# Tile 0's lists move into the step loop, the second batch's lists ahead of it, and an output tile goes behind the sum

## The chip, the cores and the metric

The kernel runs on one core of a Trainium2 chip. The metric is the device time in microseconds of one execution. Before the change it is 549.84 us, the median of 3 runs (545.92, 549.84, 549.85). The execution that was profiled took 548.86 us, of which 547.1 us lie between the first and the last instruction.

## The reference

One layer of a graph transformer over 4096 nodes of 256 features. The mask is sparse (adjacency plus the diagonal) and its density falls with the node number, so tile 0 (nodes 0 to 127) has by far the most neighbours.

```python
mask = adj.astype(float32) + eye(n)
q = (h @ Wq.T + bq).reshape(n, 8, 32)      # k and v the same way
scores = einsum('nhd,mhd->hnm', q, k) / sqrt(32)
scores = where(mask == 0, -1e9, scores)
ctx = einsum('hnm,mhd->nhd', softmax(scores), v).reshape(n, 256)
h1 = layer_norm(h + ctx @ Wo.T + bo)
ff = relu(h1 @ W1.T + b1) @ W2.T + b2      # 256 -> 1024 -> 256
h2 = layer_norm(h1 + ff)
```

## The kernel before, in words

**Stages.** The kernel first projects keys and values of all 4096 nodes on TensorE, 16 pairs of tiles (`project_kv`), and stores them to a table in HBM through the POOL and ACT queues. Queries are projected pair by pair (`project_q`) and stored to 16 small tables by the SP queue. Meanwhile VectorE looks for the neighbours in the adjacency rows (`find_dve` for most tiles, `find0_dve` for tile 0). A neighbour list is a few slots for each unit, a range of columns; neighbours beyond the slots spill to rows of other partitions.

**Batches and steps.** Every batch but tile 0's is one step of the loop over `STEPS`: 19 steps, the first four with one tile each, then pairs of tiles in steps 4 to 15, then three single tiles in 16 to 18. b0 and b1 are the first two batches. Tile 0 (`TILE0`, 14 units) is not a step: its pieces are spread over later steps (gathers from step 6, scores in steps 8 to 14, softmax in step `SOFTMAX0` = 15, weights in `WEIGHTS0` = 16, its sum in `SUM0` = 17).

**Lists.** Before a batch can gather, a chain over three engines makes its spill lists: `spill_dve`, then `starts_pe` (one small matmul), `distance_act`, `rt_dve`, `lists_pe` (one matmul for each unit), `cols_dve`, which gives the row numbers in `col_of`; only then can the POOL queue issue `gather_edges` and `gather_queries` (indirect DMAs). In the loop, step i makes the lists of step i+1. Before the change b1's lists are made in step 0, and tile 0's lists are made whole between the projections and step 0.

**A step.** VectorE multiplies gathered queries and keys (`edge_scores_dve`, L636 to L643), then the own scores; TensorE spreads the edge scores to their rows (`ell_pe`, L850); VectorE masks and takes the maximum, ScalarE the exponential, TensorE sends tops and sums back (`tr_pe`, L858), VectorE weights the values (`edge_weight_dve`, L741), TensorE sums them (`sum_pe`, L876 and L879), ScalarE moves the context out (`ctx_act`, L989). VectorE also finds the neighbours of step i+2.

**Dense work.** From step 4 on (`FIRST_JOB`) the layers behind the attention run in the gaps of the steps, one job of four tiles for two steps. The even step (place 0) has the attention output `post_pe_attn` (L1101), the odd step (place 1) the relu halves `post_pe_ff` (L1121) and two of the four output tiles `post_pe_out` (L1134); the other two come in the even step that follows. `dense(gap)` is what a gap holds; `outs_own` says which output tiles the odd step holds and where. `post_act_x` (L1145) adds a bias to the residual of the next job and stands behind `ctx_act` in the odd step; `post_pe_attn` waits for it.

Each engine runs its own instruction list in program order; semaphores tie them together. So a wait holds up all that stands behind it on that engine.

Of the kernel before, what the change touches and what calls it, by code (L numbers as in the profile page):

```python
# [5 lines left out]
ALU = mybir.AluOpType  # L6
# [7 lines left out]
P = 128  # L14
# [72 lines left out]
def batches():  # L87
# [12 lines left out]
    for p, q in enumerate(other[:1] + [q for q in out if q.first] + other[1:]):  # L100
# [18 lines left out]
SUM0 = NB - 2  # L119

# [25 lines left out]
def build(nc, xT, adj, wqkvT, bq, bk, bqkv, woT, w1T, w2T, cols, g2, be2, out):  # L146
    with ExitStack() as ctx:
# [193 lines left out]

        psum0 = sem("psum0")
# [42 lines left out]
        def job(g, first_tile, at, bank, signals):  # L385
# [33 lines left out]
         s_gprobs, s_gpt_ps, s_gpt, s_gpv, s_grl, s_gctx, s_gctxT_ps, s_gctxT) = [sem(n) for n in (  # L419
            "s_gkt s_gmask s_gdiag s_gqt_ps s_gqt s_gscores s_gmax s_gnm "  # L420
            "s_gprobs s_gpt_ps s_gpt s_gpv s_grl s_gctx s_gctxT_ps s_gctxT").split()]
# [165 lines left out]
        def starts0_dve(dve):  # L587

            q = TILE0
            dve.wait_ge(starts_ps, q.p + 1)  # L590
            nc.vector.scalar_tensor_tensor(units(mids, q), ps[:, SMALL, 0:q.U], -2.0, units(spill, q), ALU.mult, ALU.add
                                           ).then_inc(starts_ready, 1)

        def rt_dve(dve, q):
            dve.wait_ge(distance, 2 * q.p + 1)
# [5 lines left out]
        def cols_dve(dve, q):  # L601

            got = lists_out(q)
            dve.wait_ge(lists_ps, q.p + 1)
            base = (q.tiles[0] // 2) * 2 * P
            if q.first:
                nc.vector.tensor_scalar(row_of[q.par][:, 0:q.U], got[:, :, q.k + 1], -1.0 - base, 0.0, ALU.add, ALU.max)
                nc.vector.tensor_copy(row0, got[:, :, q.k + 1])
            else:

                nc.vector.tensor_scalar(row_at[q.par][:, 0:q.U], got[:, :, q.k + 1], -0.5 - base, None, ALU.add)
            nc.vector.tensor_tensor(hot(q), slot_minus_edge[:, 0:q.k].unsqueeze(1).to_broadcast([P, q.U, q.k]),
                                    got[:, :, q.k:q.k + 1].to_broadcast([P, q.U, q.k]), ALU.is_equal).then_inc(hot_ready, 1)
            dve.wait_ge(hot_ready, 2 * q.p + 1)
            wait(dve, cols_ready, q.p)
            pick = picked[:, 0:q.U * q.k].rearrange("p (u k) -> p u k", k=q.k)
            nc.vector.tensor_tensor(pick, hot(q), got[:, :, 0:q.k], ALU.mult).then_inc(hot_ready, 1)
            dve.wait_ge(hot_ready, 2 * q.p + 2)
# [3 lines left out]
        def onehot0_dve(dve):  # L622

            q = TILE0
            dve.wait_ge(cols_ready, q.p + 1)
# [199 lines left out]
        def starts_pe(pe, q):  # L825
            pe.wait_ge(spill_ready, q.p + 1)
            wait(pe, starts_ready, q.p)
            wait(pe, distance, 2 * q.p)
            if q.b == 1 and not q.first:
                pe.wait_ge(cols_ready, TILE0.p + 1)  # L830
            nc.tensor.matmul(ps[:, SMALL, 0:q.U], minus_before[:], units(spill, q), start=True, stop=True).then_inc(starts_ps, 1)

        def lists_pe(pe, q):
            pe.wait_ge(rt_ready, q.p + 1)
            pe.wait_ge(distance, 2 * q.p + 2)
            wait(pe, cols_ready, q.p)
# [47 lines left out]
        def queries0_pe(pe, i):  # L884
# [3 lines left out]
            pe.wait_ge(rt_ready, q.p + 1)  # L888
# [38 lines left out]
        def distance_act(act, q):  # L927

            if not q.first:
# [107 lines left out]
        def gather_edges(pool, q, us=None):  # L1037
            pool.wait_ge(cols_ready, q.p + 1)
            kv_ready(pool)
            if q.first:  # L1040
                queries_ready(pool, q)
# [374 lines left out]
        def outs_own(place, gap):  # L1416
            return {(1, 3): (0, 1)}.get((place, gap), ())
# [646 lines left out]
```

## Time and profile before

| What | Value |
|---|---|
| Median of 3 runs | 549.84 us |
| Profiled execution, span | 548.86 us, 547.1 us |
| TensorE matmuls busy | 475.1 us (87%) |
| VectorE busy | 388.5 us (71%) |
| GpSimd busy | 269.2 us (49%) |
| ScalarE busy | 215.6 us (39%) |
| Mean granted TensorE clock | 0.935 |

Busy time is what an engine spent in its instructions; the granted clock is given as a share of the full 2.4 GHz, so 0.5 is 1.2 GHz. In a timeline a row is a start, a duration, engine, line, operation, shape and count; brackets give the idle time of the engine just before, and what ended it. TensorE is busy nearly always between 158 us and 426 us, and less so between 69 us and 158 us, which holds the end of the projections and steps 0 to 3.

### The profile page before, as it was taken

Reading aid. Unit: us, or ns where it says so; the run is one execution under the profiler, and the core shown is the slowest. Engines: PE = TensorE matmul, PEld = TensorE weight load, DVE = VectorE, ACT = ScalarE, POOL = GpSimd, SP = SyncE. Lnnn points to the kernel's source line nnn. Section 1 sums busy time; section 2 is a strip of 40 time slices with the busy share of each in tenths; the row PEclk is TensorE's granted clock in tenths of the full one; section 3 lists DMA queues with packets and bytes.
Section 4 is the critical chain, followed back from the end, with each engine's and each line's share of the span. In section 5 each row is a group of like instructions: output and inputs, shape, how many; then the busy total and the mean of one; then the engine's idle time right before and its main releaser. Section 6 shows DMA issues by size and latency. Waiting matters only on the chain.

```text
span 547.1 us, 7365 instructions
## 1 busy us (share of the span) xinstructions
PE 475.1 (87%) x2274; PEld 373.5 (68%) x2274; DVE 388.5 (71%) x1067; ACT 215.6 (39%) x533; POOL 269.2 (49%) x374
## 2 busy tenths in 40 slices
PE   5999959588266989999999999999999499989893
PEld 4888858476255478668758857957856487668682
DVE  0258837479968687889989989998978779653103
ACT  1234243324223533633562463362463434422530
POOL 7544342435414526677656667645546264600502
PEclk9999978989557998999999999999999789999997
DMA  7999748969997979999998998994856323310101
GB/s 179 295 269 324 214 162 192 192 197 237 211 285 135 250 133 192 226 163 241 177 222 196 133 228 170 193 222 111 189 142 118 91 88 112 92 40 1 40 0 42
DMA packets 42571, 91.66 MB, mean 168 GB/s; under 512 B 4888, under 2 KB 20632, under 8 KB 42400
## 3 DMA queue, kind: packets, MB, share of 16 engines
q0 software_dynamic: 16512, 55.60, 52.9%
q1 hardware_dynamic: 24224, 33.69, 17.7%
q10 hardware_dynamic: 1792, 1.85, 1.0%
q8 instruction: 20, 0.33, 0.2%
q14 instruction: 23, 0.19, 0.1%
HBM read 123.09 MB, written 16.80 MB: 256 GB/s over the span
## 4 chain that ended last, share of the span: by engine, by line
PE 56%; DVE 15%; issue 9%; DMA 8%; POOL 5%; ACT 5%; SPq 1%; POOLq 0%; ACTq 0%; DVEq 0%
PE ps L1121 16%; PE ps L1134 14%; DMA xT_all<-in_xT 6%; PE ps L1101 6%; PE ps L1796 5%; PE ps L1089 2%; DVE slots L732 2%; PE ps L876 2%; DVE adj_bytes L531 2%; PE ps L1812 2%; PE ps L850 2%; DVE adj_bytes L535 2%; PE ps L879 1%; DMA work<-q_table,row_of 1%; POOL slots L1044 1%
## 5 line engine op out<-in xcount | busy, mean ns | idle before, releaser
L1134 PE MATMUL ps<-w,xT_all 128*128 128x256 f32 x512 | 118.8, 385 | 4.3 <-ACT xT_all L1171 2.6
L1121 PE MATMUL ps<-xT_all,w 128*128 128x512 f32 (+1 forms) x288 | 117.9, 554 | 2.6 <-ACT xT_all L1171 1.4
L1134 PEld LDWEIGHTS ps<-w,xT_all 128*128 128x128 f32 x512 | 96.0, 192 | 18.0 <-ACT xT_all L1171 3.8
L1044 POOL DMA_INDIRECT slots<-kv_table,col_of x54 | 52.7, 977 | 91.0 <-DVE col_of L620 75.0
L1121 PEld LDWEIGHTS ps<-xT_all,w 128*128 128x128 f32 x288 | 52.3, 192 | 47.2 <-issue 40.1
L1034 POOL DMA_INDIRECT slots<-kv_table,found x48 | 50.6, 1055 | 44.0 <-PE ps L879 21.0
L1171 ACT ACTIVATE xT_all<-ps,col_table 128x512 f32<-128x512 f32 (+1 forms) x72 | 45.8, 641 | 59.2 <-PE ps L1121 58.3
L1796 PE MATMUL ps<-early,xT_all 128*128 128x256 f32 x256 | 59.4, 393 | 6.9 <-DMA early<-in_wqkvT 6.3
L1796 PEld LDWEIGHTS ps<-early,xT_all 128*128 128x128 f32 x256 | 49.7, 197 | 14.8 <-DMA xT_all<-in_xT 4.7
L531 DVE MAX8 adj_bytes<-adj_bytes 128x8 f32<-128x1024 f32 (+5 forms) x40 | 38.2, 974 | 16.1 <-DMA adj_bytes<-in_adj 16.1
L1052 POOL DMA_INDIRECT work<-q_table,row_of x40 | 42.3, 1058 | 13.8 <-issue 13.8
L1191 DVE BATCH_NORM_STATS2 stats<-ps 128x6 f32<-128x256 f32 x62 | 22.2, 419 | 29.8 <-PE ps L1089 29.8
L1101 PE MATMUL ps<-wo,xT_all 128*128 128x256 f32 x128 | 39.6, 438 | 4.1 <-issue 4.1
L989 ACT ACTIVATE xT_all<-ps,col_table 128x256 f32<-128x256 f32 (+1 forms) x38 | 14.4, 431 | 70.1 <-PE ps L879 70.0
L535 DVE FIND_INDEX8 adj_bytes<-adj_bytes 128x8 uint32<-128x1024 f32 (+5 forms) x40 | 39.0, 981 | 0.0
L1230 POOL TENSOR_TENSOR rstd<-mv,eps_col 128x4 f32<-128x4 f32 (+1 forms) x17 | 5.8, 342 | 67.2 <-DVE mv L1197 66.8
L1812 PE MATMUL ps<-early,xT_all 128*128 128x256 f32 x128 | 37.7, 421 | 1.1 <-ACT slots L1647 1.1
L876 PE MATMUL ps<-work,slots 128*128 128x128 f32 x160 | 29.0, 293 | 10.3 <-DVE slots L741 8.5
L1557 POOL TENSOR_TENSOR slots<-slots,early 128x512 f32<-128x512 f32 x16 | 20.2, 1263 | 30.7 <-ACT slots L1647 30.7
L876 PEld LDWEIGHTS ps<-work,slots 128*128 128x128 f32 x160 | 24.6, 205 | 12.0 <-DVE slots L741 9.9
L1647 ACT COPY slots<-ps 128x1024 f32<-128x1024 f32 x16 | 16.2, 1012 | 41.6 <-PE ps L1796 41.6
L1101 PEld LDWEIGHTS ps<-wo,xT_all 128*128 128x128 f32 x128 | 25.6, 222 | 7.2 <-issue 4.6
(178 smaller groups left out, 854.9 us busy)
## 6 DMA issues: line engine op xcount, KB each, us to landing
adj_bytes<-in_adj POOLq DMA_DIRECT2D x31, 512.0 KB
kv_table<-slots POOLq DMA_DIRECT2D x7, 1024.0 KB, 12.8
xT_all<-in_xT SPq DMA_DIRECT2D x13, 512.0 KB, 31.5
slots<-kv_table SPq DMA_DIRECT2D x12, 512.0 KB
out_dram<-early SPq DMA_DIRECT2D x7, 512.0 KB
q_own<-q_table SPq DMA_DIRECT2D x12, 256.0 KB
slots<-in_adj SPq DMA_DIRECT2D x1, 2048.0 KB, 24.8
q_table<-slots SPq DMA_DIRECT2D x8, 256.0 KB, 6.6
```

What stands on the lines that cost most here:

```text
L531: nc.vector.max(top_words[:, u, :], words[:, lo:hi]).then_inc(hunt, 1)
L535: last = nc.vector.max_index(word_at[:, u, :], top_words[:, u, :], words[:, lo:hi])
L876: nc.tensor.matmul(to, edge_slots(q)[:, c, feats], onehot[q.par][:, c, :], start=(u == 0), stop=False)
L1034: nc.gpsimd.indirect_dma_start(to, None, kv_dram, bass.IndirectOffsetOnAxis(ap=idx, axis=0)).then_inc(got_aligned[q.par], 16)
L1044: nc.gpsimd.indirect_dma_start(edge_slots(q)[:, u, :], None, kv_dram, bass.IndirectOffsetOnAxis(ap=col_of[q.par][:, u:u + 1], axis=0)).the ...
L1052: nc.gpsimd.indirect_dma_start(q_edge[q.par][:, u, :], None, q_dram[q.no // 2], bass.IndirectOffsetOnAxis(ap=row_of[q.par][:, u:u + 1], ax ...
L1101: nc.tensor.matmul(to, q["ctxT"][:, k, j * P:(j + 1) * P], wo[:, k, :], start=(k == 0), stop=False)
L1121: last = nc.tensor.matmul(ps[:, q["bank"] + f % 2, 0:q["g"] * P], w1[:, k, f * P:(f + 1) * P], q["h1T"][:, k, :], start=(k == 0), stop=(k ...
L1134: nc.tensor.matmul(to, q["ffT"][:, f, j * P:(j + 1) * P], w2[:, f, :], start=(f == 0), stop=False)
L1171: nc.scalar.activation(q["ffT"][:, f, :], ps[:, q["bank"] + f % 2, 0:q["g"] * P], ACT.Relu, bias=bias_1[:, f:f + 1]).then_inc(q["ff"], 1)
L1796: last = nc.tensor.matmul(ps[:, kv_bank(i, part), j * D:(j + 1) * D], xT_all[:, c, k, r * P:(r + 1) * P], wqkv[:, k, (1 + part) * D:(2 + p ...
L1812: nc.tensor.matmul(to, xT_all[:, c, k, r * P:(r + 1) * P], wqkv[:, k, 0:D], start=(k == 0), stop=False)
```

## The change

Five things are changed. (1) b1's lists are made during the projections, so that the gathers of b0 and b1 are issued one after the other. (2) Tile 0's lists are made in steps 3 (`LISTS0`) to 5 with a semaphore of their own, `lists0`, and in another PSUM bank; VectorE's search of tile 0 stays where it was. (3) `project_q(0)` goes behind the last `project_kv`, and one adjacency load goes from step 0 to the projections. (4) In odd steps the second of two output tiles goes behind `sum_pe`. (5) Tile 0's softmax goes ahead of the search in step 15, its `tr0_pe` to the end of step 15, half of its weighting and both halves of its sum to step 17.

```diff
-    for p, q in enumerate(other[:1] + [q for q in out if q.first] + other[1:]):
+    for p, q in enumerate(other[:2] + [q for q in out if q.first] + other[2:]):
+LISTS0 = 3
         def outs_own(place, gap):
-            return {(1, 3): (0, 1)}.get((place, gap), ())
+            return {(1, 3): (0,), (1, 4): (1,)}.get((place, gap), ())
@@ sync @@
             load_own(sp, STEPS[0])
-            sp.wait_ge(got_edges[STEPS[0].par], 2 * STEPS[0].U * 16)
-            store_q(1)
             load_own(sp, STEPS[1])
-            for i in range(2, Q_BEFORE):
+            for i in range(1, Q_BEFORE):
                 store_q(i)
@@ gpsimd @@
-                if c == 4:
-                    load_adj(pool, c)
+                if c in (4, 6):
+                    load_adj(pool, STEPS[4].h + c // 6)
             gather_aligned(pool, STEPS[0])
+            gather_edges(pool, STEPS[1])
+            gather_queries(pool, STEPS[1])
+            gather_aligned(pool, STEPS[1])
...
-                if i == 0:
-                    load_adj(pool, STEPS[4].h + 1)
@@ scalar @@
-                if i == 13:
-                    take_q(0)
-            distance_act(act, TILE0)
+                if i == 12:
+                    distance_act(act, b1_)
+                    mask_act(act, b1_)
             store_kv(PAIRS - 2)
             store_kv(PAIRS - 1)
+            take_q(0)
+            rows_act(act, b1_)
+            onehot_act(act, b1_)
...
+                if i == SOFTMAX0:
+                    probs0_act(act)
                 edge_exp_act(act, q)
...
                 ctx_act(act, q)
-                if i == SOFTMAX0:
-                    probs0_act(act)
...
+                if i == LISTS0:
+                    distance0_act(act)
@@ tensor @@
-                if i == 13:
-                    project_q(0)
+                if i == 11:
+                    starts_pe(pe, b1_)
                 if i == 14:
-                    starts_pe(pe, TILE0)
-            for i in range(1, Q_LISTS):
-                project_q(i)
-            lists_pe(pe, TILE0)
-            project_q(Q_LISTS)
-            starts_pe(pe, b1_)
-            for i in range(Q_LISTS + 1, Q_BEFORE):
+                    lists_pe(pe, b1_)
+            for i in range(Q_BEFORE):
                 project_q(i)
...
+                if i == LISTS0:
+                    starts0_pe(pe)
...
                 starts_pe(pe, STEPS[i + 2])
+                if i == LISTS0 + 1:
+                    lists0_pe(pe)
+                if i == SOFTMAX0:
+                    tr0_pe(pe)
...
-                if i == SUM0:
-                    sum0_pe(pe, 0)
...
+                tr_pe(pe, q)
                 if i == SUM0:
-                    sum0_pe(pe, 1)
-                if i == WEIGHTS0:
-                    tr0_pe(pe)
-                tr_pe(pe, q)
+                    for k in range(KC):
+                        sum0_pe(pe, k)
@@ vector @@
+                if i == 3:
+                    find_dve(dve, b1_, 0)
+                    columns_dve(dve, b1_)
+                    spill_dve(dve, b1_)
...
+                if i == 12:
+                    rt_dve(dve, b1_)
                 if i == 13:
                     listed0_dve(dve)
                     spill_dve(dve, TILE0)
-            find_dve(dve, b1_, 0)
-            starts0_dve(dve)
-            columns_dve(dve, b1_)
-            spill_dve(dve, b1_)
+            cols_dve(dve, b1_)
             find_dve(dve, STEPS[2], 0)
-            rt_dve(dve, TILE0)
-            cols_dve(dve, TILE0)
-            onehot0_dve(dve)
...
+                if i == LISTS0:
+                    starts0_dve(dve)
                 norm_probs_dve(dve, q)
+                if i == WEIGHTS0 + 1:
+                    weight0_dve(dve, 1)
+                if i == SOFTMAX0:
+                    own0_dve(dve)
+                    below0_dve(dve)
...
+                if i == SOFTMAX0:
+                    norm0_dve(dve)
                 edge_below_dve(dve, q)
                 own_sum_dve(dve, q)
                 edge_weight_dve(dve, q)
-                if i == SOFTMAX0:
-                    own0_dve(dve)
-                    below0_dve(dve)
+                if i == LISTS0 + 1:
+                    rt0_dve(dve)
+                if i == LISTS0 + 2:
+                    cols0_dve(dve)
                 if i == WEIGHTS0:
                     weight0_dve(dve, 0)
-                    weight0_dve(dve, 1)
...
-                if i == SOFTMAX0:
-                    norm0_dve(dve)
```

The POOL queue behind the last key and value store, before the change. `col_of` rows are edge gathers, `row_of` query gathers, `found` rows the gathers of a tile's own first slots.

```order
L1044 DMA slots<-kv_table,col_of 128x512 x2
L1052 DMA work<-q_table,row_of 128x256 x2
L1034 DMA slots<-kv_table,found 128x512 x4
L1070 DMA adj_bytes<-in_adj 128x4096
L1044 DMA slots<-kv_table,col_of 128x512 x2
L1052 DMA work<-q_table,row_of 128x256 x2
L1070 DMA adj_bytes<-in_adj 128x4096
```

The same place of the POOL queue after the change.

```order
L1093 DMA slots<-kv_table,col_of 128x512 x2
L1101 DMA work<-q_table,row_of 128x256 x2
L1081 DMA slots<-kv_table,found 128x512 x2
L1093 DMA slots<-kv_table,col_of 128x512 x2
L1101 DMA work<-q_table,row_of 128x256 x2
L1081 DMA slots<-kv_table,found 128x512 x2
L1119 DMA adj_bytes<-in_adj 128x4096
```

b1's edge and query gathers now stand directly behind b0's, and only one adjacency load is left among them.

VectorE in step 15, from the reciprocal of the step's own softmax on, before the change. `scores` rows of 1800 elements are tile 0's.

```order
L698 TENSOR_TENSOR own_p<-scores,top_rec 128x2x8x2
L531 MAX adj_bytes<-adj_bytes 128x8 x3
L535 MAX_INDEX adj_bytes<-adj_bytes 128x8 x3
L710 TENSOR_TENSOR p_edge<-s_edge,ps 128x16
L719 TENSOR_TENSOR slots<-slots,own_p 128x4x256
L732 TENSOR_TENSOR slots<-slots 128x2x256
L738 SCALAR_TENSOR_TENSOR p_edge<-p_edge,ps 128x16
L741 TENSOR_TENSOR slots<-slots,p_edge 128x2x256
L778 TENSOR_TENSOR slots<-slots,q_own 128x256
L780 TENSOR_REDUCE scores<-slots 128x8
L787 TENSOR_REDUCE top_rec<-scores 128x8
L789 TENSOR_TENSOR scores<-scores,top_rec 128x1800
```

The same place after the change.

```order
L746 TENSOR_TENSOR own_p<-scores,top_rec 128x2x8x2
L826 TENSOR_TENSOR slots<-slots,q_own 128x256
L828 TENSOR_REDUCE scores<-slots 128x8
L835 TENSOR_REDUCE top_rec<-scores 128x8
L837 TENSOR_TENSOR scores<-scores,top_rec 128x1800
L533 MAX adj_bytes<-adj_bytes 128x8 x3
L537 MAX_INDEX adj_bytes<-adj_bytes 128x8 x3
L843 TENSOR_REDUCE total_p<-scores 128x8
L845 RECIPROCAL top_rec<-total_p 128x8
L847 TENSOR_TENSOR scores<-scores,top_rec 128x8
L758 TENSOR_TENSOR p_edge<-s_edge,ps 128x16
L767 TENSOR_TENSOR slots<-slots,own_p 128x4x256
```

Tile 0's softmax now stands ahead of the step's own weighting of values (L741 before; L789 now, three rows behind this excerpt), for which `sum_pe` waits.

## Rows read from the trace of the kernel before

**Rows 1.** The page: busy time of TensorE, and the chain that ended last.

```profile
PE 475.1 (87%) x2274; PEld 373.5 (68%) x2274; DVE 388.5 (71%) x1067; ACT 215.6 (39%) x533; POOL 269.2 (49%) x374
PE 56%; DVE 15%; issue 9%; DMA 8%; POOL 5%; ACT 5%; SPq 1%; POOLq 0%; ACTq 0%; DVEq 0%
```

**Rows 2.** Busy by stretch: engines, TensorE clock, DMA share, GB/s.

```profile
124.00:158.00 34.00, 17.17 (x90) 14.65 (x89) 29.89 (x83) 12.45 (x41) 15.49 (x17) 0.70 1.02 248
...
250.00:295.00 45.00, 43.39 (x216) 32.96 (x216) 41.49 (x97) 20.52 (x52) 30.69 (x32) 1.00 0.95 199
...
426.00:458.00 32.00, 24.33 (x135) 21.53 (x134) 25.97 (x61) 12.03 (x30) 12.81 (x14) 0.84 0.31 91
```

**Rows 3.** VectorE's timeline: end of tile 0's lists, steps 0 to 4.

```profile
84.22 2.83 DVE L627 TENSOR_SCALAR work<-row_mid,adj_bytes 128x128 f32<-128x128 f32 x14
86.97 0.68 DVE L636 TENSOR_TENSOR work<-work,slots 128x512 f32<-128x512 f32 x1
...
101.08 0.23 DVE L580 SCALAR_TENSOR_TENSOR idx_all<-found,row_ids 128x16 f32<-128x16 uint32 x1
107.04 0.69 DVE L636 TENSOR_TENSOR work<-work,slots 128x512 f32<-128x512 f32 x1 [5.73 <-DMA work<-q_table,row_of]
...
123.07 0.69 DVE L636 TENSOR_TENSOR work<-work,slots 128x512 f32<-128x512 f32 x1 [0.58 <-DMA work<-q_table,row_of]
...
156.84 0.69 DVE L636 TENSOR_TENSOR work<-work,slots 128x512 f32<-128x512 f32 x1 [2.55 <-DMA work<-q_table,row_of]
```

**Rows 4.** POOL's timeline: first and last gathers of b0, b1 and step 2.

```profile
76.08 1.10 POOL L1044 DMA_INDIRECT slots<-kv_table,col_of  x1 [5.14 <-DMA kv_table<-slots]
...
95.49 0.99 POOL L1044 DMA_INDIRECT slots<-kv_table,col_of  x1 [8.91 <-DVE col_of L620]
...
99.43 1.42 POOL L1052 DMA_INDIRECT work<-q_table,row_of  x1 [0.30 <-issue]
...
119.26 1.05 POOL L1052 DMA_INDIRECT work<-q_table,row_of  x1 [0.30 <-issue]
```

**Rows 5.** TensorE's timeline: tile 0's 28 list matmuls, and 28 of its sum.

```profile
76.60 6.16 PE L838 MATMUL ps<-first_idx,work 128*128 128x18 f32 x28 [4.53 <-DVE work L598]
...
467.72 3.37 PE L920 MATMUL ps<-work,slots 128*128 128x128 f32 x28
```

**Rows 6.** VectorE in step 5, then TensorE's first attention output in step 6.

```profile
184.70 0.52 DVE L598 TENSOR_SCALAR work<-work,spill 128x128 f32<-128x128 f32 x2 [2.21 <-ACT idx_all L941]
...
187.90 0.16 DVE L611 TENSOR_SCALAR row_at<-ps 128x2 f32<-128x2 f32 x1 [1.76 <-PE ps L838]
...
193.50 0.17 DVE L710 TENSOR_TENSOR p_edge<-s_edge,ps 128x16 f32<-128x16 f32 x1 [1.73 <-PE ps L858]
...
205.03 1.10 PE L1101 MATMUL ps<-wo,xT_all 128*128 128x256 f32 x4 [1.59 <-issue]
```

**Rows 7.** ScalarE's residual bias, and TensorE's attention output in steps 8 and 14.

```profile
249.85 1.33 ACT L1145 ACTIVATE xT_all<-xT_all,col_table 128x512 f32<-128x512 f32 x2
251.28 1.10 PE L1101 MATMUL ps<-wo,xT_all 128*128 128x256 f32 x4 [1.18 <-issue]
...
384.59 1.10 PE L1101 MATMUL ps<-wo,xT_all 128*128 128x256 f32 x4 [0.32 <-issue]
```

**Rows 8.** Steps 15 and 16: VectorE, then TensorE.

```profile
412.51 1.34 DVE L531 MAX8 adj_bytes<-adj_bytes 128x8 f32<-128x112 f32 x3
...
420.48 2.03 DVE L787 TENSOR_REDUCE top_rec<-scores 128x8 f32<-128x1800 f32 x1
...
428.64 2.03 DVE L795 TENSOR_REDUCE total_p<-scores 128x8 f32<-128x1800 f32 x1 [2.62 <-ACT scores L995]
...
417.20 3.72 PE L1134 MATMUL ps<-w,xT_all 128*128 128x256 f32 x16 [0.43 <-ACT xT_all L1171]
...
433.39 1.53 PE L850 MATMUL ps<-work 128*128 128x56 f32 x6 [7.08 <-DVE work L643]
```

**Rows 9.** Busy by stretch, columns as in rows 2: behind that idle time.

```profile
433.00:439.00 6.00, 5.61 (x22) 4.80 (x22) 4.41 (x11) 0.37 (x1) 0.00 (x0) 0.56 0.00 0
```

More of the change, by code:

```diff
@@ L340, in build @@
         got_edges = [sem(f"got_edges{i}") for i in range(SETS)]
+        lists0 = sem("lists0")
         psum0 = sem("psum0")
@@ new lines, in distance0_act, with rt0_dve @@
+        def distance0_act(act):
+            q = TILE0
+            act.wait_ge(lists0, 2)
+            for u in range(q.U):
+                last = nc.scalar.activation(rt[q.par][:, u, :], edge_mid, ACT.Abs, bias=mids[:, q.u0 + u:q.u0 + u + 1], scale=-2.0)
+            last.then_inc(lists0, 1)
+            nc.scalar.copy(lists(q)[:, :, q.room], ps[:, ELL2, 0:q.U]).then_inc(lists0, 1)
+        def rt0_dve(dve):
+            q = TILE0
+            dve.wait_ge(lists0, 4)
+            for u in range(q.U):
+                row = rt[q.par][:, u, :]
+                last = nc.vector.tensor_scalar(row, row, spill[:, q.u0 + u:q.u0 + u + 1], None, ALU.is_lt)
+            last.then_inc(lists0, 1)
@@ new lines, in lists0_pe, with cols0_dve @@
+        def lists0_pe(pe):
+            q = TILE0
+            pe.wait_ge(lists0, 5)
+            for u in range(q.U):
+                last = nc.tensor.matmul(lists0_out()[:, u, :], rt[q.par][:, u, :], lists(q)[:, u, q.A:q.room + 2], start=True, stop=True)
+            last.then_inc(lists0, 1)
+        def cols0_dve(dve):
+            q = TILE0
+            got = lists0_out()
+            dve.wait_ge(lists0, 6)
+            base = (q.tiles[0] // 2) * 2 * P
+            nc.vector.tensor_scalar(row_of[q.par][:, 0:q.U], got[:, :, q.k + 1], -1.0 - base, 0.0, ALU.add, ALU.max)
+            nc.vector.tensor_copy(row0, got[:, :, q.k + 1])
+            nc.vector.tensor_tensor(hot(q), slot_minus_edge[:, 0:q.k].unsqueeze(1).to_broadcast([P, q.U, q.k]),
+                                    got[:, :, q.k:q.k + 1].to_broadcast([P, q.U, q.k]), ALU.is_equal).then_inc(lists0, 1)
+            dve.wait_ge(lists0, 7)
+            dve.wait_ge(cols_ready, LISTS0 + 4)
+            pick = picked[:, 0:q.U * q.k].rearrange("p (u k) -> p u k", k=q.k)
+            nc.vector.tensor_tensor(pick, hot(q), got[:, :, 0:q.k], ALU.mult).then_inc(lists0, 1)
+            dve.wait_ge(lists0, 8)
+            with nc.allow_low_precision(reason="one whole number below 4096 and zeros"):
+                nc.vector.tensor_reduce(col_of[q.par][:, 0:q.U], pick, AX_X, ALU.add).then_inc(lists0, 1)
+            dve.wait_ge(lists0, 9)
@@ L1972, in _ @@
                 own_scores_dve(dve, q)
-                if soon:
+                if soon and i > 0:
                     rt_dve(dve, soon)
```

109 lines of the change are left out of this document (56 added, 53 removed).

## The prediction, made before the changed kernel had run

> **What bounds the kernel now.** I read the page first: TensorE is busy 475.1 us of 547.1 and holds 56% of the chain that ended last [rows 1]. The table by stretch says that this is two regimes. From step 8 to 12 TensorE has 43.4 us busy in 45 and VectorE 41.5, at full clock [rows 2]: TensorE sets the pace and VectorE is close behind. In steps 2 and 3 (124 to 158 us) TensorE has 17.2 in 34, VectorE 29.9, and the DMA engines are full (share 1.02). So in front of step 4 the chain of lists, gathers and VectorE sets the pace, and what is saved there moves everything behind it; from step 4 on an added TensorE microsecond costs one. A third stretch, 426 to 458 us, has TensorE at 24.3 in 32 and a clock of 0.84.
>
> **1. The hand-over to the steps.** Before, step 0 starts on VectorE at 86.97 without idle time, right behind the 2.83 us of tile 0's one-hot rows [rows 3]: tile 0's lists hold it, not b0's data. Step 1 starts at 107.04, 5.73 of idle behind the end of step 0 at 101.31, since b1's `col_of` comes out of step 0: POOL idles 8.91, issues b1's gathers from 95.49 to 100.85 (99.43 and 1.42) and they land 6.2 later [rows 4].
>
> Now b0's first gather goes out between 73.9 (one query pair of 2.2 us of TensorE is taken out of the last projections) and 76.1 (no gain: the moved adjacency load shares the DMA engines with the last store); I take 75.3. Four gathers at about 1.25 us (99.43 is the fourth from 95.49, each 0.95 to 1.4 and a gap of 0.30) end at 80. The landing behind the last issue is 2.7 in step 2 (119.26 and 1.05, VectorE at 123.07) and 6.2 in step 1 [rows 3, 4]. b0's gathers go out ahead of the step loop's own loads, so I take the short one: step 0 starts at 82.5 instead of 86.97. Step 0 took 14.3 us and loses b1's `rt` and `cols` (1.1 us with their wait of 1.6 on TensorE, of which the wait for `tr_pe` gives most back): 13.5, so it ends at 96. b1's gathers are then all issued by 87 and landed by 93 even with 6.2, so step 1 starts at 96, 11 earlier. From step 1 on the old chain holds again (`cols`, gathers, landing): step 1 to step 2 was 16.0 us, and the wait in its middle for a TensorE at half clock is shorter now, so I take 15. Steps 2 and 3 keep their 33.8 (123.07 to 156.84). Step 4 starts at 144.8: **12.1 us earlier**. Ends: 8 if the full DMA queues of rows 2 give a third back, 14 if step 3 does not wait its 2.55 [rows 3].
>
> The Trainium skill ("Trainium Kernel Development and Optimization", Key Constraints) says that DMAs issued from SP, ACT and POOL share the same 16 engines and interleave. By that rule the adjacency load that now stands in front of the last stores slows them, and the first gather goes out no earlier than before, which would take 0.8 of the 12.1; no row here shows that load beside those stores.
>
> b1's search on VectorE (about 4.4 us) goes into the idle time in front of tile 0's search and costs nothing while its adjacency rows are there by then; if not, tile 0's search moves, which has no reader until step 3 now.
>
> **2. Tile 0's lists on TensorE.** They took 6.16 us for 28 matmuls at half clock, behind 4.53 of idle: free where they stood. At full clock 28 matmuls of tile 0's sum take 3.37 [rows 5]. They now stand at the end of step 4 where TensorE is the bound, with one small matmul in step 3: **+3.2**. ScalarE's 14 distances (some 4.4 us) come at the end of step 3, where it waits anyway; VectorE's `rt` of 2.83 in step 4 is taken up by the waits of step 5, 2.21 + 1.76 + 1.73 [rows 6].
>
> **3. Tile 0's columns on VectorE.** `cols0` is 1.45 us and again 2.83 of one-hot rows, 4.3 together, behind the last work of step 5. From `tr_pe` of step 5 (VectorE goes on at 193.50) to the spread scores of step 6 VectorE took 8.45 us and now needs 12.75; TensorE's own work over the same stretch is 9.4, so it waits 3.4. Before, it waited 2.2 there for the bias (1.59 in the row, the rest around `ell_pe`) [rows 6], and that wait goes by part 4. With the extra 0.7 of waking up: **+1.9**. Late next: the edge gathers of step 7, by as much, covered by step 6's 3 us of waits.
>
> **4. An output tile behind the sum.** Before, `ctx_act` and the 1.33 us of residual bias run while TensorE has nothing left but `ell_pe`: the bias ends at 251.18 and the attention output starts at 251.28, after 1.18 of idle; in step 14 0.32 is left [rows 7] (four such rows, steps 8 to 14, 2.5 together). Now one output tile of 3.6 us of TensorE covers them. `edge_weight_dve` is ready some 1.1 us before the first output tile ends in steps 7 to 13, so `sum_pe` does not wait where it now stands: **-2.5**.
>
> **5. Steps 15 to 17.** Before, TensorE idles 7.08 in front of step 16, because VectorE sits 2.62 at tile 0's sum of exponentials for ScalarE, which is behind `ctx_act` [rows 8]. That wait goes. But VectorE now reaches `edge_weight_dve` of step 15 only at: 412.5, own scores 0.9, top and subtraction 4.1 (2 x 2.03), search 2.8 (maxima 1.34, indices as much), sums 2.4, and 2.8 of the step's own, 425.5. TensorE is through with the one output tile at 417.20 + 3.6 = 420.8, so it **waits 4.7 in the odd step instead of 7.08 in the even one**. The second output tile (3.6) and `tr0_pe` (3.1) follow, `ell_pe` of step 16 comes at 434 to 436 where it was at 433.39, but 3.1 of work is done already. In step 17 `tr_pe` had half of tile 0's sum to cover its wait; now nothing does (2.8), and the sum waits for the second half of the weighting (1.5). Added up to `sum_pe` of step 17, I get +0.6 if TensorE stays at full clock behind the 4.7 of idle and +2.8 if it falls: **+1.5**. Behind the 7.08 the granted clock was 0.56, nearly the lower level, for the next 6 us [rows 9].
>
> The Trainium skill ("TensorE: Matmul & The Clock Gate", Why this matters for your kernels) advises against idle gaps between bursts of matmuls since they bring the clock back to half. By that rule the sum takes +2.8 for this part. The trace agrees for the gap of 7.08 (0.56 behind it).
>
> **Sum.** -12.1 + 3.2 + 1.9 - 2.5 + 1.5 = -8.0, from 548.86 to 540.9. The profiled execution is 0.98 below the median of the runs, so against the median I say **541.8**.
>
> **The rivals.**
> (a) *The gain is larger*, 0.16: step 3 is rid of its wait for data (14 instead of 12.1), VectorE's waits in step 6 take up `cols0`, and steps 15 to 17 come out even: 549.84 - 14 + 3.2 - 2.5 = 536.5. For it: the waits of rows 6. Against: DMA share 1.02.
> (b) *Small gain*, 0.24: 9 from the hand-over, 3.5 lost at the end with the clock down, and the gaps of part 4 come back as waits for VectorE, which has only 3.5 in 45 to spare [rows 2]: 549.84 - 9 + 3.2 + 1.9 - 1 + 3.5 = 548.4, up to 545 with parts of it.
> (c) *DMA holds the hand-over*, 0.10: b1's gathers now stand in one burst with b0's, and with the queries' stores and w1 and w2 (1 MB each) the queues of rows 2 stay as full, so that step 4 comes only 4.5 earlier, what step 0 gains: 549.84 - 4.5 + 3.2 + 1.9 - 2.5 + 1.5 = 549.4.
> (d) *Slower*, 0.05: VectorE becomes the bound. Tile 0's 2.83 + 4.3 = 7.1 in steps 4 and 5 are then wholly exposed, TensorE waits for spread scores in every even step after, and nothing of part 4 comes. It decides if VectorE's waits in steps 5 and 6 are under 3 together. With (c)'s 4.5: 549.84 - 4.5 + 3.2 + 7.1 + 2.8 = 558.4. Against: 5.7 of waits in step 5 alone [rows 6].
> (e) My forecast, 0.45: 539 to 544.3. A change that does not do what it says can only be the split of part 4 (if VectorE is late for the sum by over a microsecond, TensorE stands where it did not); it is in (b).
>
> **Range and chances.** 80% lie between 536 and 549: it leaves out (d), half of (c) and the far end of (a). A measurement here tells about 1% from no change, 5.5 us. Faster (under 544.3): (e), (a) and a little of (b), 0.65. Within: 0.30. Slower: 0.05.
>
> **What the profile will show.** Right: step 0 on VectorE near 82.5, step 1 near 96 without a wait for data, step 4 near 145; 28 list matmuls of about 3.2 us at the end of step 4; TensorE waiting about 3 us ahead of step 6; no idle at the attention output in steps 8 to 14; TensorE idle 4 to 5 us at `sum_pe` of step 15 and none ahead of step 16. Wrong: step 1 still waiting for gathers; VectorE's waits gone between step 6 and step 14; or a clock under 0.95 between 250 and 400 us.

## The result, and the profile after

The changed kernel takes 550.9 us (median of 15; 549.56 to 552.2), the kernel before 548.08 beside it (545.16 to 550.0): ratio 1.0048, 95% interval 1.003 to 1.0066. It is not 8 us faster but half a per cent slower. The profiled execution took 552.0, with a span of 549.8. Busy times on the page rose a little, TensorE's by 1.9:

```profile
PE 477.0 (87%) x2274; PEld 375.0 (68%) x2274; DVE 389.5 (71%) x1067; ACT 216.6 (39%) x533; POOL 271.4 (49%) x374
...
PE 58%; DVE 18%; issue 8%; ACT 5%; POOL 5%; DMA 4%; POOLq 0%; ACTq 0%; DVEq 0%
```

The busy times do not show where the gain went, so I compared starts. Each column is the start of the named work of that step, from the timelines of VectorE (edge scores) and TensorE (`ell_pe`):

| Kernel | VectorE step 0 | step 1 | step 4 | TensorE `ell` 4 | 6 | 7 | 15 | 16 | 18 |
|---|---|---|---|---|---|---|---|---|---|
| before | 87.0 | 107.0 | 156.8 | 158.7 | 202.8 | 227.8 | 405.7 | 433.4 | 488.4 |
| after | 87.5 | 102.0 | 150.5 | 152.3 | 203.6 | 226.8 | 401.9 | 432.6 | 491.0 |
| load back | 82.0 | 96.3 | 144.3 | 146.1 | 197.6 | 220.8 | 395.9 | 426.7 | 485.1 |
| before + split | 86.3 | 107.2 | 157.7 | 159.5 | 203.5 | 225.0 | 400.2 | 425.5 | 481.3 |
| tail back | 87.7 | 102.1 | 149.1 | 150.9 | 203.1 | 224.9 | 400.0 | 425.3 | 480.4 |

The changed kernel is 6.3 ahead at step 4 (12 forecast), 0.8 behind at `ell` of step 6, 1.0 ahead at step 7, 3.8 ahead at step 15, and 2.6 behind at step 18. From there to the end both take 58.7 to 58.8.

**Hand-over.** POOL and VectorE, in answer to [rows 3, 4]. POOL's first gather is b0's; VectorE's first row is the start of step 0, its last the start of step 1:

```profile
68.26 1.26 POOL L1604 TENSOR_TENSOR slots<-slots,early 128x512 f32<-128x512 f32 x1 [2.63 <-ACT slots L1695]
77.91 1.08 POOL L1093 DMA_INDIRECT slots<-kv_table,col_of  x1 [8.39 <-DMA kv_table<-slots]
```

```profile
87.52 0.69 DVE L684 TENSOR_TENSOR work<-work,slots 128x512 f32<-128x512 f32 x1 [18.14 <-DMA work<-q_table,row_of]
...
95.81 0.29 DVE L741 TENSOR_REDUCE total_p<-scores 128x8 f32<-128x136 f32 x1 [3.18 <-ACT scores L1023]
...
102.01 0.68 DVE L684 TENSOR_TENSOR work<-work,slots 128x512 f32<-128x512 f32 x1
```

Step 1 has no wait for data any more, as forecast. But POOL sat 8.39 for the last stores of k and v, so that the first gather came at 77.9, behind both ends of the forecast (73.9 to 76.1), and VectorE 18.14 for b0's queries.

**Tile 0's lists.** TensorE from the end of step 4 to step 6, in answer to [rows 5, 6]:

```profile
174.26 3.28 PE L653 MATMUL ps<-first_idx,work 128*128 128x18 f32 x28
...
201.67 0.38 PE L879 MATMUL ps<-spill,minus_before 128*128 128x2 f32 x2 [1.45 <-DVE spill L579]
...
203.56 0.65 PE L898 MATMUL ps<-work 128*128 128x48 f32 x4 [1.50 <-DVE work L691]
```

The 28 matmuls cost 3.28 (3.2 forecast). The two waits, 2.95 together, stand behind VectorE's one-hot rows at the end of step 5 (3.4 forecast).

**The tail.** TensorE in step 15, in answer to [rows 8], then in step 17:

```profile
421.67 0.79 PE L924 MATMUL ps<-work,slots 128*128 128x128 f32 x2 [4.33 <-DVE slots L789]
...
424.39 4.94 PE L1183 MATMUL ps<-w,xT_all 128*128 128x256 f32 x16
...
429.52 3.28 PE L956 MATMUL ps<-top_rec,work 128*128 128x16 f32 x28
432.65 0.85 PE L898 MATMUL ps<-work 128*128 128x56 f32 x6
...
465.74 1.46 PE L906 MATMUL ps<-top_rec,work 128*128 128x16 f32 x6 [2.75 <-DVE top_rec L743]
467.98 5.02 PE L968 MATMUL ps<-work,slots 128*128 128x128 f32 x28 [0.78 <-DVE slots L868]
```

The wait of 4.33 for the sum is the 4.7 of the forecast. The forecast had the output tile and `tr0_pe` behind it, too, but the output tile takes 4.94 where another takes 3.72, with a granted clock of 0.75 between 421.6 and 432.65. `ell_pe` of step 16 waits behind all of it, though VectorE had its input ready at 425.3 (the spreading product starts at 424.96 and takes 0.33). In step 17 TensorE now waits 1.15, 2.75 and 0.78 for VectorE where it waited 0.17 and 1.58 before, and the first half of tile 0's sum takes 5.02 where the second takes 3.29. (Tile 0's sum stood in step 17 before the change as well; what moved is that both halves now stand behind `tr_pe`.)

### The profile page after: what moved, and what is told of

It is laid out like the page before. It is cut to its first block, busy times and chain, and to the rows that moved or that the text cites. A ratio compares the mean times of both kernels' runs of the same rounds, so it can differ in the third digit from the quotient of the medians.

```text
span 549.8 us, 7362 instructions
## 1 busy us (share of the span) xinstructions
PE 477.0 (87%) x2274; PEld 375.0 (68%) x2274; DVE 389.5 (71%) x1067; ACT 216.6 (39%) x533; POOL 271.4 (49%) x374
## 4 chain that ended last, share of the span: by engine, by line
PE 58%; DVE 18%; issue 8%; ACT 5%; POOL 5%; DMA 4%; POOLq 0%; ACTq 0%; DVEq 0%
PE ps L1170 15%; PE ps L1183 12%; PE ps L1848 10%; PE ps L1150 5%; DVE adj_bytes L537 3%; DVE adj_bytes L533 3%; PE ps L924 2%; PE ps L1138 2%; DMA work<-q_table,row_of 2%; PE ps L898 2%; PE ps L968 1%; POOL slots L1093 1%; PE ps L1864 1%; PE ps L1160 1%; DMA kv_table<-slots 1%
## 5 line engine op out<-in xcount | busy, mean ns | idle before, releaser
L1081 POOL DMA_INDIRECT slots<-kv_table,found x48 | 52.2, 1087 | 54.7 <-DVE found L554 25.4
L924 PE MATMUL ps<-work,slots 128*128 128x128 f32 x160 | 30.3, 301 | 13.1 <-DVE slots L789 13.1
L898 PE MATMUL ps<-work 128*128 128x56 f32 (+1 forms) x80 | 13.4, 298 | 18.3 <-DVE work L691 14.2
```

The costliest lines, as they stand in the source:

```text
L924: nc.tensor.matmul(to, edge_slots(q)[:, c, feats], onehot[q.par][:, c, :], start=(u == 0), stop=False)
L1081: nc.gpsimd.indirect_dma_start(to, None, kv_dram, bass.IndirectOffsetOnAxis(ap=idx, axis=0)).then_inc(got_aligned[q.par], 16)
```

## Experiments

All were timed beside the kernel before, whose median was 547.7 to 548.6 in the four groups (single runs 542.9 to 551.6). In brackets stand the ratio to it and its 95% interval. "Shift" is against the changed kernel's 550.9, which was timed in another group: a microsecond of a shift can be that. A profile is one execution; starts and waits are read from it, times from the medians.

### The adjacency load back in step 0

```diff
-                if c in (4, 6):
-                    load_adj(pool, STEPS[4].h + c // 6)
+                if c == 4:
+                    load_adj(pool, c)
...
+                if i == 0:
+                    load_adj(pool, STEPS[4].h + 1)
```

> The changed kernel with one edit: the adjacency load that it moved in front of the last two stores of k and v (for step 5's batch) goes back to where it stood, in step 0. Changed kernel: 550.9 us median, first gather of b0 at 77.9, step 0 on VectorE at 87.5. Theory A (that load shares the DMA engines with the last stores and holds the first gather): first gather at about 75.3, step 0 at 85, step 1 at 99.5, everything behind 2 to 2.6 earlier, 548.5. Theory B (the stores are slow by themselves or by what the queues hold anyway): first gather stays at 77.5 to 78, time 550.5 to 551.5; it may be up to 1 slower, since the load then stands among the early gathers.

Measured: 546.07 (ratio to before 0.9958, 0.9929 to 0.9987), shift -4.8. Theory A, and more than it said:

```profile
kv_table<-slots ACTq DMA_DIRECT2D x2, 512.0 KB, 2.8
```

```profile
72.61 1.08 POOL L1093 DMA_INDIRECT slots<-kv_table,col_of  x1 [3.71 <-DMA kv_table<-slots]
```

The first of these is the DMA issues of 55 to 92 us in this kernel: ScalarE's two stores land after 2.8 each (last column: median us from issue to landing). In the changed kernel the same row says 7.7. The first gather goes out at 72.6 instead of 77.9, step 0 starts at 82.0, step 1 at 96.3, step 4 at 144.3. The forecast had 82.5, 96 and 144.8.

### The adjacency load behind the last bias

```diff
             bias_k(PAIRS - 1)
+            load_adj(pool, STEPS[4].h + 1)
             gather_edges(pool, STEPS[0])
```

> The changed kernel with one edit: the adjacency load issued on POOL behind its last bias of k (about 69.5) instead of in front of the last two biases (63.2); the stores of ScalarE go out at 67 to 70. In the changed kernel these stores of 256 KB take 7.7 from issue to landing and b0's first gather starts at 77.9; with the load put back in step 0 they take 2.8, gather 72.6, step 0 at 82.0, 546.07. Theory A (the 512 KB share the DMA engines with whatever is on the way): the last store still has to share, first gather at 75 to 78, 548 to 551. Theory B (it counts who was issued first: the stores queue behind the load): stores at 3 to 4, first gather at 73 to 74, but the load then runs beside b0's gathers: 546 to 548.

Measured: 550.51 (1.0063, 1.0035 to 1.0092), shift -0.4. The first gather comes at 77.22, in the range of theory A. But POOL issues the load at 68.77, between the two stores (66.48 and 68.86), and the two fare differently:

```profile
kv_table<-slots ACTq DMA_DIRECT2D x1, 512.0 KB, 2.8
```

```profile
kv_table<-slots ACTq DMA_DIRECT2D x1, 512.0 KB, 7.5
```

The first of these is the DMA issues of 66 to 68.5 us, the second those of 68.5 to 70.9 (each store is 512 KB, not the 256 of the expectation): the store ahead of the load lands after 2.8, the store 0.09 behind it after 7.5. In the changed kernel, where the load is issued 3.9 ahead of the first store and 6.3 ahead of the last, they take 7.9 and 7.5. So 6.2 us less of a lead over the last store bought nothing: the first gather comes 8.4 behind that store in both kernels. Theory B's 3 to 4 for both stores did not come. Whether a load issued just behind the last store would hold it as well was not run.

### Both output tiles ahead of the sum again

```diff
-            return {(1, 3): (0,), (1, 4): (1,)}.get((place, gap), ())
+            return {(1, 3): (0, 1)}.get((place, gap), ())
```

> The changed kernel with one edit: both output tiles of an odd step ahead of the sum on TensorE again. Theory A (the split is worth what the comparison of steps 8 to 15 shows, 2.5 to 2.8): 553.5. Theory B (VectorE is late enough that the split only moves the wait, and what steps 8 to 15 gained came from elsewhere): 550.5 to 551.5. Theory C (in step 15 the split is what makes TensorE wait 4.3 for the sum, and so a loss at the end): gain of 2.5 lost over steps 7 to 14, up to 3.6 won back in step 15, 549.5 to 551.

Measured: 547.15 (0.9979, 0.9952 to 1.0007), shift -3.7. No theory had it: undoing the split makes the changed kernel faster. From `ell` of step 7 to that of step 15 it costs 3.3 (178.4 against 175.1), somewhat more than theory A says, and in step 15 it gives 6.3 back (24.4 against 30.7 to `ell` of step 16), nearly twice theory C.

### The split alone, on the kernel before

The same two lines the other way round, in the kernel before.

> The kernel before with one edit: in odd steps one of the two output tiles behind the sum on TensorE. Prediction's theory (the bias of ScalarE is covered in steps 8 to 14, 2.5): 545.6. Theory B (VectorE becomes what TensorE waits for): 547.5 to 549. Theory C (step 15 gives 1 to 3 of it back, since TensorE then reaches the sum 3.6 earlier and idles at a lower clock behind it): 546.5 to 548.

Measured: 542.1 against 548.58 (0.9881, 0.9835 to 0.9928): 6.5 us, over twice the forecast's 2.5. Steps 7 to 14 give 2.7 (177.9 to 175.2), the forecast's term. The rest is step 6 (25.0 to 21.6) and step 15 (27.7 to 25.3); ahead of step 4 and from step 16 to 18 this trace is 0.8 longer each. Step 6, before and with the split, columns as in rows 2:

```profile
202.80:209.00 6.20, 4.61 (x21) 3.81 (x20) 3.94 (x8) 3.93 (x12) 4.43 (x5) 0.77 0.73 223
209.00:215.00 6.00, 6.00 (x31) 5.18 (x31) 4.21 (x18) 1.30 (x4) 3.14 (x5) 0.95 0.93 131
```

```profile
202.80:209.00 6.20, 6.20 (x40) 5.48 (x39) 5.56 (x15) 2.88 (x12) 3.83 (x5) 1.00 0.90 256
209.00:215.00 6.00, 6.00 (x32) 5.32 (x31) 5.93 (x14) 2.44 (x6) 4.76 (x8) 1.00 0.95 135
```

Behind the 1.59 of idle ahead of the attention output [rows 6] the granted clock falls (0.77 over this stretch), and the attention output takes 6.5 instead of 4.9: with it step 6 costs 3.4 more, not 1.59. Behind the 1.18 of step 8 [rows 7] the clock stays at 1.00.

The changed kernel has the split, but does not get this gain in full. Its own waits of 1.45 and 1.50 stand ahead of step 6, and the clock falls all the same:

```profile
202.80:209.00 6.20, 5.44 (x22) 4.48 (x23) 5.38 (x10) 1.32 (x6) 4.45 (x4) 0.72 0.57 155
```

Its step 6 takes 23.3. Nine traces have these same two waits: in eight the attention output then takes 6.5, in the ninth (the tail in its old order, below) 5.0. So the fall is frequent behind such a gap, not certain.

### The tail in its old order

```diff
-                if i == SOFTMAX0:
-                    own0_dve(dve)
-                    below0_dve(dve)
...
                 edge_weight_dve(dve, q)
+                if i == SOFTMAX0:
+                    own0_dve(dve)
+                    below0_dve(dve)
```

and likewise `norm0_dve`, `probs0_act`, `tr0_pe`, the second half of the weighting and the two halves of `sum0_pe`.

> The changed kernel with the order of steps 15 to 17 as before the change: tile 0's own scores, maxima, exponentials and sums behind VectorE's weighting of step 15, its spread softmax in step 16, its sum in two halves ahead of step 17's. Prediction's theory (this part costs 1.5): 549.4. Theory B, from the two traces (from ell of step 15 to ell of step 18 the changed kernel loses 6.4): 544.5 to 545.5. Theory C (the loss is that of a TensorE that got ahead of VectorE by 3.8 and gives it back in whatever order the tail stands, since VectorE's own work sets the tail): 550 to 551.

Measured: 543.05 (0.9904, 0.9867 to 0.9942), shift -7.9. Theory B, and more. `ell` of step 16 comes 25.3 behind that of step 15 instead of 30.7, `ell` of step 18 55.1 behind that of step 16 instead of 58.4. TensorE idles 4.78 ahead of step 16 here and still is 5.4 better off:

```profile
425.34 1.53 PE L898 MATMUL ps<-work 128*128 128x56 f32 x6 [4.78 <-DVE work L691]
```

It starts step 16 as soon as VectorE has the spread scores; in the changed kernel VectorE has them at the same time and TensorE does 7.4 of other work first.

### The split undone in step 15 alone

```diff
-                        post_pe_out(pe, now, n, outs_own(place, gap))
+                        post_pe_out(pe, now, n, outs_own(place, gap) if i != SOFTMAX0 else {3: (0, 1)}.get(gap, ()))
```

> The changed kernel with one edit: in step 15 alone both output tiles stand ahead of the sum on TensorE again; steps 7 to 13 keep the split. Changed kernel 550.9. Theory A (in step 15 the tile behind the sum is the loss: TensorE idles 4.33 for the weighting that now stands behind tile 0's softmax on VectorE, then has the second tile and tile 0's spreading still to do before step 16): ell of step 16 comes 30.7 behind ell of step 15 in the changed kernel and 24.4 with the split undone everywhere; so 5 to 6 faster, 545.5. Theory B (VectorE sets step 16 anyway and TensorE only trades one wait for another): 550 to 551. Prediction's theory (a wait of 4.7 here in place of 7.08 there, all in all +1.5): at most 1.5 faster, 549.4.

Measured: 544.93 (0.9941, 0.9916 to 0.9966), shift -6.0. Theory A. Both tiles run at full clock while VectorE works, and nothing but `tr0_pe` is left behind the sum:

```profile
421.38 0.49 PE L924 MATMUL ps<-work,slots 128*128 128x128 f32 x2 [0.65 <-DVE slots L789]
...
422.95 3.28 PE L956 MATMUL ps<-top_rec,work 128*128 128x16 f32 x28
426.08 1.02 PE L898 MATMUL ps<-work 128*128 128x56 f32 x6
```

### Tile 0's weighting and sum in their old place

```diff
-                if i == WEIGHTS0 + 1:
-                    weight0_dve(dve, 1)
...
                     weight0_dve(dve, 0)
+                    weight0_dve(dve, 1)
...
                 ell_pe(pe, q)
+                if i == SUM0:
+                    sum0_pe(pe, 0)
```

(and `sum0_pe(pe, 1)` ahead of `tr_pe`).

> The changed kernel with one edit: in steps 16 and 17 tile 0's weighting in one piece in step 16 and its sum on TensorE in two halves ahead of step 17's spreading, as before the change; step 15 stays as changed. With the whole tail undone the time falls from 550.9 to 543.05, of which ell of step 16 to ell of step 18 has 3.3 (58.4 against 55.1) and ell of step 15 to ell of step 16 5.4. Theory A (the two places are separate losses): 547.6. Theory B (all of the loss is step 15's, steps 16 to 18 only follow from it): 550 to 551. Theory C (all of it is the sum's, through the clock, 0.79 between 465 and 480): 544 to 545.

Measured: 546.25 (0.9972, 0.9947 to 0.9997), shift -4.65: theory A, somewhat more. Step 16 takes 1.5 longer than in the changed kernel and step 17 5.6 less. The sum fills step 17's wait for VectorE, and the clock stays up. The stretch from `ell` of step 17 to `tr_pe`, here and in the changed kernel (there without the sum, which follows at 0.75):

```profile
460.00:469.40 9.40, 9.36 (x72) 8.41 (x73) 5.38 (x17) 7.34 (x20) 5.01 (x5) 1.00 0.25 66
```

```profile
458.70:467.90 9.20, 4.60 (x21) 3.10 (x19) 6.67 (x19) 7.29 (x20) 5.63 (x6) 0.82 0.45 128
467.90:475.00 7.10, 7.02 (x48) 7.02 (x49) 7.00 (x7) 0.22 (x1) 6.61 (x4) 0.75 0.20 59
```

### Load and tail back together, and tile 0's lists elsewhere

> The changed kernel with two edits: the adjacency load back in step 0, and the order of steps 15 to 17 as before the change. Alone they gave 4.8 and 7.9. If they add up: 550.9 - 12.7 = 538.2, which would beat the kernel before with the split alone (542.1). If the front and the tail pull at the same time (VectorE's or ScalarE's own chain at the end does not move): 541 to 543.

Measured: 536.69 (0.9806, 0.9772 to 0.984). They add up: a shift of -14.2, against -12.7 for the sum of the two.

With `LISTS0 = 2` on top:

> As the kernel with the adjacency load and the tail order put back, and tile 0's lists one step earlier (small matmul and starts in step 2, distances behind it, the 14 comparisons and the 28 list matmuls at the end of step 3, columns and one-hot rows in step 4). Where they stand in the changed kernel, steps 4 and 5 took 51.3 from ell of step 4 to ell of step 6 against 44.1 before. Theory A (in step 3 TensorE idles and in step 4 VectorE waits 3.3 and TensorE 5.0, so most of the 7.2 is hidden): 4 to 6 faster than that kernel, 532 to 534. Theory B (VectorE sets steps 1 to 3, so 2.8 of comparisons move step 4 by 2.8, and the 4.3 of columns hold the spread scores of step 5): within 1.5 of it. A loss of 2 if the gathers of step 4 come later too.

Measured: 535.2 (0.9778, 0.9746 to 0.981), 1.5 better: the edge of theory B. Step 4 starts little later on VectorE (144.8 against 144.3), but `ell` of step 4 comes 4.9 later, as the comparisons and list matmuls stand ahead of it, and by step 6 it is 2.5 ahead. No wait stands ahead of step 6 and the clock stays up there, so that it is 4.2 ahead by step 7. The profiled execution, the fastest of its six, is 5 better; the medians do not show that much.

With the one-hot rows in step 6 instead, `LISTS0` as changed:

```diff
+                if i == GATHER0:
+                    onehot0_dve(dve)
```

> As the kernel with the adjacency load and the tail order put back (536.69), and the 14 one-hot rows of tile 0 (2.83 of VectorE) behind the weighting of step 6 instead of step 5. There TensorE waits 1.45 and 1.50 at the end of step 5, at 2.95 for the search's spill and the spread scores behind those rows. Theory A (these two waits are the one-hot rows'): both gone in step 5, ell of step 4 to ell of step 6 at 48 instead of 51.3, 534 if step 6 has room. Theory B (they only move on, VectorE has no room in step 6 either): the waits turn up ahead of step 7, 536 to 537.

Measured: 535.21 (0.9743, 0.9708 to 0.9778). Theory A in step 5 (the waits of 1.45 and 1.50 shrink to one of 0.34; `ell` 4 to `ell` 6 takes 47.6 instead of 51.5), though 1.17 turns up ahead of step 7. Of the 7.1 that tile 0's lists cost in steps 4 and 5, 3.9 is these rows. What is left of that at the end is 1.5 by the medians, 3.4 by the ratios to the kernel before.

### Split and tail, all four combinations

The two edits undone together in the changed kernel, and the new tail without and with the split in the kernel before.

> The changed kernel with the order of steps 15 to 17 as before and both output tiles ahead of the sum. With this run the four combinations on the changed kernel are complete: both 550.9, tail undone 543.05, split undone 547.15. Theory A (the split is worth 6 with the old tail, and the new tail without it is no loss): 549. Theory B (the new tail costs 7.9 whatever the split does, and the split costs 3.7 whatever the tail does): 539.3. Theory of the prediction (split -2.5, tail +1.5, independent): 552.

> The kernel before (548.1 to 548.6) with the new order of steps 15 to 17 alone. Theory A (no loss without the split; TensorE's 7.08 of idle ahead of step 16 goes, and the sum of tile 0 without cover in step 17 costs 4.65 of it): 546.5 to 548.5. Theory B (the new tail is bad by itself): 553 to 556. Prediction: 550.

> The kernel before with the new order of steps 15 to 17 and the split. Theory A (together they cost what they cost in the changed kernel, 7.9 over the split alone at 542.1): 550. Theory B (independent terms as measured on the kernel before): 542.1 plus what the new tail alone does there. Prediction: 547.5.

Measured: 547.42 (0.9989, 0.9962 to 1.0015), 546.8 (0.9996, 0.9967 to 1.0024) and 547.0 (1.0009, 0.9977 to 1.004), beside 547.67 for the kernel before. Medians:

| | old tail | new tail |
|---|---|---|
| changed kernel, tiles ahead of the sum | 547.42 | 547.15 |
| changed kernel, split | 543.05 | 550.9 |
| kernel before, tiles ahead | 547.7 to 548.6 | 546.8 |
| kernel before, split | 542.1 | 547.0 |

The new tail without the split is no loss on either (-0.3, -0.9, neither clear of noise); the split with the old tail gains 4.4 and 6.5; together they lose 3.5 against neither in the changed kernel, and are even in the kernel before. That is 8.2 and 6.7 worse than the two parts added up: theory A in kind, and neither "bad by itself" nor "independent". Its 550 for the last was 3 too high. I had carried the 7.9 over; there it is 4.9 by the medians, which are of different groups, and 7.0 by the ratios to the kernel before.

That the new tail alone is even hides two parts. Without the split, `ell` of step 15 to that of step 16 takes 24.4 with the new tail and 27.7 with the old one, on both kernels; but step 16 to step 18 takes 58.0 and 60.8, where the old tail takes 55.0 and 55.2. So the early softmax is a gain in step 15, and what it gains is lost again by step 18, where the sum has lost its cover (putting it back in the changed kernel gave 4.65). The wait is the same in the kernel before with both, though:

```profile
417.72 0.79 PE L876 MATMUL ps<-work,slots 128*128 128x128 f32 x2 [4.33 <-DVE slots L741]
```

### The best of it

Load back, split undone in step 15 alone, weighting and sum back, `LISTS0 = 2`; tile 0's softmax and `tr0_pe` stay in step 15 as changed.

> The changed kernel with four edits: adjacency load back in step 0 (-4.8 alone), both output tiles ahead of the sum in step 15 alone (-6.0 alone), tile 0's weighting in one piece and its sum in halves ahead of step 17's spreading (-4.65 alone), tile 0's lists one step earlier (-1.5 on top of others). If all add up: 550.9 - 17 = 534. The kernel with the whole tail order put back and the lists a step earlier has 535.2; theory A (softmax of tile 0 early in step 15 is as good once the tile behind the sum is gone there): 533 to 535. Theory B (the edits of step 15 and of the sum buy the same idle time, as the whole tail's 7.9 is less than their 10.6): 536 to 538.

Measured: **531.96** (0.9691, 0.965 to 0.9733), 16.6 below the kernel before, better than every other. Theory A.

> As the kernel with those four edits, and the one-hot rows of tile 0 in step 6. With the lists a step earlier VectorE does these rows in step 4, where TensorE waits for ScalarE's normalization anyway. Theory A (they are hidden in step 4, and are not in step 6, where TensorE has full work): 0 to 2 slower than without. Theory B (they hold step 5's gathers or spread scores in step 4): 1 to 2.8 faster.

Measured: 532.86 (0.9702, 0.9669 to 0.9734), 0.9 slower: in theory A's range, and no difference that these runs can tell.

And the best with GpSimd's two instructions of step 17 (`post_pool_gain`, `post_pool_final`) behind `if i == S + 2` instead of `S + 1`:

> The best kernel (531.96: load back, split undone in step 15 alone, weighting and sum back, tile 0's lists a step earlier) with GpSimd's product and sum over 128x1024 of step 17 in step 18. VectorE's three additions there take 5.9 instead of 1.3 beside them. Theory A (this is on the path: VectorE's weighting holds the sum of step 17, where TensorE waits 1.6): 1.5 to 4 faster, 528 to 530.5, and the additions at 1.3. Theory B (TensorE's own work sets the end, or the two instructions now slow VectorE in step 18): 531 to 533.

Measured: 531.97 (0.9738, 0.9698 to 0.9778). Inconclusive: in GpSimd's program nothing stands between the two places that it waits for, so both instructions ran where they had, and VectorE's additions still took 5.94:

```profile
452.89 5.94 DVE L780 TENSOR_TENSOR slots<-slots 128x256 f32<-128x256 f32 x3
```

## Why the prediction was wrong

The terms of the sum, each with what the two traces show for its stretch of the kernel:

| Term | Forecast | Measured | From |
|---|---|---|---|
| 1 hand-over, step 4 | -12.1 | -6.3 | start of step 4, 156.8 to 150.5 |
| 2 and 3, tile 0's lists | +5.1 | +5.4 | `ell` 4 to `ell` 7: 69.1 to 74.5 |
| 4 split | -2.5 | -2.8 | `ell` 7 to `ell` 15: 177.9 to 175.1 |
| 5 tail | +1.5 | +6.4 | `ell` 15 to `ell` 18: 82.7 to 89.1 |
| behind step 18 | 0 | +0.1 | `ell` 18 to the end |
| Sum | -8.0 | +2.8 | medians +2.8, spans +2.7 |

Two steps failed: part 1 by 5.8 and part 5 by 4.9. Together they are the whole miss.

**Part 1, the last store.** I priced the adjacency load beside the last stores at 0.8 and left it out of the sum. It cost 5.3 at the first gather, 6.2 at step 4 and 4.8 of the time. The rest of the part held: 82.0, 96.3 and 144.3 with the load back. (Two sizes in it were off against each other: the first gather could go out at 72.6 instead of 75.3, and b0's queries landed 4.5 behind their last issue instead of 2.5.) The rule of the Trainium skill ("Trainium Kernel Development and Optimization", Key Constraints), that all issuers' DMAs share 16 engines and interleave, had the sign right. The traces agree: the two stores take 2.8 each without the load, 7.9 and 7.5 with it in front of both, and 2.8 and 7.5 with it between them. Rival (c), step 4 only 4.5 earlier by DMA, was nearest to what came, but blamed the burst of gathers, the queries' stores and the weights.

**Part 5, the tail.** By step:

| Step | Forecast's terms | Measured |
|---|---|---|
| 15 | +0.6 to +2.6 | +3.1 |
| 16 | -3.1 (`tr0_pe` done already) | -2.2 |
| 17 | +2.8 and +1.5 | +5.6 |

(`ell` of step 17 starts at 461.6 before and 458.7 after.) Each came out worse than its term, with the low clock behind the 4.33 and behind the waits of step 17 (4.94 and 5.02 for what takes 3.7 and 3.3 at full clock). And the terms add up to 1.8 to 3.8, not to the 0.6 to 2.8 that I wrote and took 1.5 from. In step 17 the old order had tile 0's sum as cover for a wait, and putting it back gives 4.65.

Under that lies a choice that I never priced. In the sum, parts 4 and 5 are two terms, and part 4 gives the split nothing in step 15, where with the old tail it gains 2.3. With the new tail VectorE is late for the sum, and the split puts an output tile (4.94 at the lower clock) behind that late sum, in front of the one product that VectorE waits for next. Without the split both tiles run at full clock in what is now the wait (0.65 of idle left); without the new order the sum is not late. Either edit alone costs nothing that these runs can tell, or gains; the pair costs 7 to 8 more than its parts. The split undone in step 15 alone gives 6.0 of it back.

**Parts 2 and 3.** They held, in part by luck. The list matmuls were right (3.28 for 3.2), and the wait ahead of step 6 nearly (2.95 for 3.4). The 0.7 of "waking up" stands on no row. What the traces show instead is an attention output of step 6 that takes 6.5 at the lower clock and 4.9 at the full one, 1.7 more; but it took 6.5 in the kernel before as well, behind the 1.59, so that it cancels.

**Part 4.** Steps 7 to 14 gave 2.8 in the changed kernel and 2.7 in the kernel before (2.5 forecast), without idle at any attention output, as I said. What I did not see is what step 6 is worth: I priced its 1.59 at its length, and with the clock it is 3.4, of which the late one-hot rows left the changed kernel half (25.0 to 23.3). The Trainium skill ("TensorE: Matmul & The Clock Gate", Why this matters for your kernels) warns of longer idle gaps than these; here the clock fell behind 1.59 (0.77) and not behind 1.18 (1.00), and the measurement decides.

Of the signs that I named, "TensorE idle 4 to 5 at `sum_pe` of step 15 and none ahead of step 16" came true in a kernel that was slower: it did not tell the two outcomes apart.

## What to carry to other kernels

Before a transfer is moved, look at which store or load ends last there, and whether the moved one is on the way at that time; here 512 KB ahead of a last store cost as much as all that the rest of the hand-over still gained. When two reorderings meet in one step, price them together: ask which instruction the other engine waits for, and what both edits together put in front of it. When a forecast has failed, compare stretches that hold a term whole: cut at step 6, tile 0's lists cost 7.1 and look like a third miss; cut at step 7, where the wait that they replaced has also passed, they cost 5.4, and 5.1 was forecast.

## What was not expected of the hardware

VectorE's three sums of own slots in step 17 take 424, 2994 and 2458 ns (5.94 in all), in step 16 1.34 together for the same three of the same shape. Beside the two slow ones POOL has a product and a sum over 128x1024:

```profile
469.25 5.94 DVE L780 TENSOR_TENSOR slots<-slots 128x256 f32<-128x256 f32 x3
```

```profile
470.06 2.35 POOL L1288 TENSOR_TENSOR early<-early,row_g 128x1024 f32<-128x1024 f32 x1
472.49 2.42 POOL L1292 TENSOR_TENSOR early<-early,row_be 128x1024 f32<-128x1024 f32 x1
```

It is 4.6 us more of VectorE in step 17, before and after the change alike (5.95 before). The Trainium skill ("GPSIMD Engine Reference", Key points) names contention of the two engines for their SBUF interfaces when VectorE's instruction has two SBUF inputs; the trace agrees, as far as the same time shows it. What it costs is open: the one attempt to move GpSimd's instructions left them where they were.
